# A cross-attention and feed-forward kernel: x is also loaded transposed and normed on VectorE in that layout

## The chip, the cores and the metric

The kernel runs on one core of a Trainium2 chip. The metric is the device time of one execution in microseconds (us). TensorE (PE) multiplies matrices, VectorE (DVE), ScalarE (ACT) and GpSimd (POOL) work element by element, and SyncE (SP) issues most of the DMA transfers.

## The reference, cut to what matters

```python
x = x + xattn(layernorm(x), ctx, ctx, gate_w, gate_b, outnorm_w)   # x, ctx: (16, 256, 256)
x = x + ffn(layernorm(x), w1, w2, h1, h2, w3, ...)
def layernorm(x):
    m = mean(x, -1); v = var(x, -1)
    return (x - m) / sqrt(v + 1e-5)
# xattn: q = layernorm(x), k = v = ctx, 8 heads of 32; input and forget gates from
#   [q, k, v] @ gate_w.T, a decay matrix from the gates (cumulative sum, running maximum),
#   scores = q k^T / sqrt(32) * decay; h = scores @ v / denominator; rms norm per head
# ffn: silu(x w1) * (x w2), then two layers gelu(h @ H) of 1024 x 1024, then w3 back to 256
```

## The kernel before

The 16 sequences are worked off as eight pairs of 512 tokens. `batch(i)` runs the feed-forward part of pair i: `swiglu` (w1 and w2), the first hidden layer (layer 0, eight column groups m), the second hidden layer (layer 1, again eight groups) and `project` (w3). Between its matrix products it carries two more stages: the attention of pair j = i + 1, and the preparation of pair g = i + 2 (first norm, transposition, gate products, scans). So the preparation runs in six batches, for the pairs 2 to 7; the pairs 0 and 1 ("plain") are prepared in a prologue of their own, and the last two batches have none.

Every hidden product is made twice, with a high part of the activations (a copy in a rounded 32-bit format, made by ScalarE) and a low part (the difference, made by VectorE: `lo(i, layer, m)`, line L1169). The product of layer 1 over chunk k needs `lo(i, 0, k)`.

The order on each engine is the order in which the program is written; engines meet only at semaphores. In a batch that prepares pair g the places that matter are these, in the order of time:

- VectorE, in the loop over m of layer 0: after `lo(i,0,3)` the statistics of x of pair g (tile `z`, tokens on partitions: 128 partitions x 4 token tiles x 256 features), after `lo(i,0,4)` the reciprocal root and the norm itself (L901, `z` in place), after m = 5 `take_state`, after m = 6 `take_far` (L1016), which waits for TensorE's `read_state` (L1539, the product of the transposed queries `zT` of pair j with the state).
- After `lo(i,0,7)` VectorE has `take_num` (L1023) and then one long chain for pair j: `mix_divide` (L1104 on), `mix_square`, `mix_rsqrt`, `residual`, the statistics of the second norm, `lo(i,1,0)`, `lo(i,1,1)`, the second norm, `lo(i,1,2)`, and `add_gate_low` (L926), which gives ScalarE the gates of pair g.
- ScalarE makes the tanh and the softplus of the gates (L633 to L645), with two table loads, and only then `gelu(1,4)` and its high part (L757). VectorE takes `lo(i,1,4)`, the running maximum (L953) and the offsets (L960 to L962) behind that.
- TensorE turns `z` of pair g into PSUM within layer 1, after chunk k = 3 (`turn_z`, eight products of 128 x 128, L1341, with `ident` and `z`). After the last group of layer 1 stand `turn_z2(j)` (L1341 again, with `num`) and `turn_rows(g)` (L1469), which waits for the offsets of the scan (L962), and behind them `project` (L1641, L1642).
- ScalarE copies the turned z to `zT` (L616) and again as its high part `normed_hi` (L622). GpSimd makes the low parts `keys_lo` (L549) and `normed_lo` (L553).

Six such batches have a period of 90.9 us each.

Of the kernel before, what the change touches and what calls it, by code (L numbers as in the profile page):

```python
# [7 lines left out]
ALU = mybir.AluOpType  # L8
ACT = mybir.ActivationFunctionType
AX = mybir.AxisListType  # L10
F32 = mybir.dt.float32
# [4 lines left out]
P = 128  # L16
# [54 lines left out]
SMAT_STEPS = W * ROWGRP  # L71


def build(nc, x, ctx_tok, ctx_t, gate_w, gate_b, outnorm_w, w_cols, scales, w3_s, out):
    with ExitStack() as stack:
        def sb(name, shape, dt=F32):
            return stack.enter_context(nc.sbuf_tensor(name, shape, dt))

        def sem(name):
            return stack.enter_context(nc.semaphore(name))  # L80

        x1_kept = nc.dram_tensor("x1_kept", [PAIRS, P, Q, DIM], F32, kind="Internal").ap()
        m_rows = nc.dram_tensor("m_rows", [BH, SEQ], F32, kind="Internal").ap()

        wgt = sb("wgt", [P, COLS], F32R)
        h_hi = [sb(f"h_hi{n}", [P, KH, NT], F32R) for n in range(2)]
# [43 lines left out]
        stats = sb("stats", [P, Q, 6])  # L130
        mv = sb("mv", [P, Q, 2])
        minus_mean = sb("minus_mean", [P, Q])
        nw = sb("nw", [P, 4, Q])
        rms = sb("rms", [P, 4, Q * HEADS])
        den = sb("den", [P, 2, Q * HEADS])
# [60 lines left out]
        s_ctxT = [sem(f"s_ctxT{n}") for n in range(2)]  # L196
        s_v = sem("s_v")
        s_norm1 = sem("s_norm1")
        s_z = sem("s_z")
        s_zT = sem("s_zT")  # L200
        s_zTe = sem("s_zTe")
# [54 lines left out]
        def first(j):  # L256
            return isinstance(j, int) and j == 0

        def zT(j):
            return work[:, 0:CH] if first(j) else zT_buf[:]  # L260

        def ctxT(j):
            return work[:, CH:2 * CH] if first(j) else ctxT_buf[:]

        def plain(j):

            return j < W
# [88 lines left out]
        @block.sync  # L356
        def _(sp):
            def load_z(j):
                sp.wait_ge(s_zT, j)
                sp.dma_start(z[:], x[j]).then_inc(s_zin, 16)  # L360

            def load_ctxT(j):
                reuse(sp, s_qk, W * j if j > 1 else 0)
                sp.dma_start(ctxT(j), ctx_t[j]).then_inc(s_ctxT[j % 2], 16)

            def load_v(j):
                reuse(sp, s_pv, Q * j)
                reuse(sp, s_kwt, j)
                sp.dma_start(v_aug[:], ctx_tok[j]).then_inc(s_v, 16)
# [63 lines left out]
            for i in range(PAIRS):  # L433
                j, g = i + 1, i + 2
                if j < PAIRS and j > 1:
                    load_x(j)
                if g < PAIRS:
                    load_z(g)
                    load_ctxT(g)
                    load_v(g)  # L440
                if j < PAIRS:
                    keep_x1(j)
                if g < PAIRS:
                    keep_rows(g)
                    spread_max(g)
                if i == PAIRS - 2:
                    for n in range(COMPARED_BEFORE_LAST + RAW):
                        load_raw(n)
                if i == PAIRS - 1:
                    for n in range(COMPARED_BEFORE_LAST + RAW, UNITS):  # L450
                        load_raw(n)
                    store_last(i)
                else:
                    store(i)
# [32 lines left out]
        def _(pool):  # L487
# [36 lines left out]
            def weigh_keys(j):  # L524

                pool.wait_ge(s_ecols, j + 1)
                pool.wait_ge(s_v, 16 * j + 16)
                reuse(pool, s_z2T, j)
                for b in range(W):
                    w = e_cols[:, 0, 1, b * HEADS:(b + 1) * HEADS].rearrange("p (h o) -> p h o", o=1).to_broadcast([P, HEADS, DH])  # L530
                    last = pool.tensor_tensor(k_wt[:, b], v_aug[:, b * TILES, :, 0:DH], w, ALU.mult)
                last.then_inc(s_kwt, 1)
# [11 lines left out]
                    dst = gained.rearrange("p (q h d) -> p q h d", q=Q, h=HEADS)[:, q]  # L544
                    pool.tensor_tensor(dst, src, gain, ALU.mult).then_inc(s_gained, 1)

            def split_keys_low(j):
                pool.wait_ge(s_keys_hi, j - W + 1)
                pool.tensor_tensor(keys_lo, ctxT(j), keys_hi.bitcast(F32), ALU.subtract).then_inc(s_keys_lo, 1)  # L549

            def split_normed_low(j):
                pool.wait_ge(s_zhi, j - W + 1)
                pool.tensor_tensor(normed_lo, zT(j), normed_hi.bitcast(F32), ALU.subtract).then_inc(s_zlo, 1)  # L553

            pool.memset(ident[:], 0.0).then_inc(s_ident, 1)
            pool.memset(head_mask[:], SCORE_SCALE).then_inc(s_ident, 1)
            pool.memset(future[:], 0.0).then_inc(s_ident, 1)
# [23 lines left out]
            pool.tensor_scalar(gain_b[:], gain_b[:], 1.0, None, ALU.add).then_inc(s_gain, 1)  # L581
            first_gain()
            load_weights((5, 6, 7, 8))
            for i in range(PAIRS):
                j, g = i + 1, i + 2
                if j < PAIRS:
                    weigh_keys(j)
                if g < PAIRS:
                    split_keys_low(g)
                    split_normed_low(g)  # L590

            def general_path(i):
                pool.sem_inc(s_alone, 1)
# [4 lines left out]
        def _(act):  # L598
# [8 lines left out]
            def take_zT(j):  # L607
                source = ps_a[:, 0:CH]
                if first(j):
                    act.wait_ge(s_zT_first, 1)  # L610
                    act.activation(zT(j)[:, 0], source[:, 0], ACT.Copy).then_inc(s_zTe_first, 1)
                    act.wait_ge(s_zT, 1)
                    act.activation(zT(j)[:, 1], source[:, 1], ACT.Copy).then_inc(s_zTe, 1)
                    return
                act.wait_ge(s_zT, j + 1)
                act.activation(zT(j), source, ACT.Copy).then_inc(s_zTe, 1)  # L616
                if plain(j):
                    return
                reuse(act, s_gate, j)
                if j >= 2:  # L620
                    act.wait_ge(s_mm, 2 * KH * (j - 2) + KH)
                act.activation(normed_hi, source, ACT.Copy).then_inc(s_zhi, 1)  # L622

            def take_gate_low(j):
                act.wait_ge(s_gate, j + 1)
# [208 lines left out]
        def _(dve):  # L834
# [78 lines left out]
            def norm_1_apply(j):  # L913
                if plain(j):
                    dve.wait_ge(s_zT, j)
                norm_apply(j, xs[j] if plain(j) else z, z, s_z)

            def norm_2_stats(j, src):
                norm_stats(s_norm2, j, src)
# [307 lines left out]
            def batch(i, a_stage, g_stage, last=False):  # L1227
                j, g = i + 1, i + 2
                for m in range(KH):
                    swiglu(i, m)  # L1230
                    if first(i) and m < W:
                        keep_first_x1(m)
                    if m >= 1:
                        lo_1(i, m - 1)
                lo_1(i, KH - 1)
                if a_stage:
                    masks(j)
                    floors(j)
                    weigh_scores(j, 0)
                for m in range(KH):  # L1240
                    lo(i, 0, m)
                    if a_stage and m == 1:
                        weigh_scores(j, 1)
                    if g_stage and m == 3:
                        norm_1_stats(g)
                    if g_stage and m == 4:
                        norm_rsqrt(s_norm1, g)
                        norm_1_apply(g)
                    if a_stage and m == 5:
                        take_state(j)  # L1250
                    if a_stage and m == 6:
                        take_far(j)
                    if a_stage and m == 7:
                        take_num(j)
                        mix_divide(j)
                    if last:
                        compare(COMPARED_BEFORE_LAST + m)
                if a_stage:
                    mix_square(j)
                    mix_rsqrt(j)  # L1260
                    residual(j)
                    norm_2_stats(j, xs[j % 2])
                for m in range(KH):
                    lo(i, 1, m)
                    if a_stage and m == 1:
                        norm_rsqrt(s_norm2, j)
                        norm_2_apply(j, xs[j % 2])
                    if g_stage and m == 2:
                        add_gate_low(g)
                    if g_stage and m == 3:  # L1270
                        scan_f(g)
                        shift_g(g)
                    if g_stage and m == 4:
                        scan_m(g)
                    if last:
                        compare(COMPARED_BEFORE_LAST + KH + m)
                    elif a_stage and not g_stage and m >= KH - COMPARED_BEFORE_LAST:
                        compare(m - KH + COMPARED_BEFORE_LAST)
                if last:
                    sum_inexact()  # L1280
                if a_stage:
                    take_z2T(j)
                if last:
                    finish_last(i)
                else:
                    finish(i)
# [50 lines left out]
        def _(pe):  # L1337
# [323 lines left out]
            def batch(i, a_stage, g_stage, as_is=False, last=False):  # L1661
# [38 lines left out]
                    pass  # L1700

                def between_3(k):
                    if g_stage and k == 3:
                        turn_z(g)

                def within_3(m):
                    pass
# [115 lines left out]
```

## Time and profile before

| | |
|---|---|
| median of 3 runs | 764.79 us (764.64 to 765.4) |
| the profiled execution, its own time | 764.41 us |
| span of its profile | 762.7 us |
| TensorE busy | 754.7 us, 99% of the span |
| VectorE busy | 543.6 us, 71% |
| ScalarE busy | 384.1 us, 50% |
| GpSimd busy | 53.7 us, 7% |
| granted TensorE clock | 0.999 of full speed |

Busy time is the time in which an engine executes instructions. TensorE's products overlap (one takes 0.39 us, the next starts 0.23 us later), so what one costs is read from the distance between starts and not from its duration. The time of an execution is 1.7 us more than its span.

### The profile page before, as it was taken

How to read it: one execution, taken by the hardware profiler on the slowest of the kernel's cores; microseconds unless marked ns; L12 is line 12 of the kernel's file. 1: busy time of each engine (PE TensorE's matmuls, PEld its weight loads, DVE VectorE, ACT ScalarE, POOL GpSimd, SP SyncE). 2: the span in 40 equal slices, each digit the busy share in tenths (PEclk: the TensorE clock that was granted, in tenths of full speed). 3: DMA queues.
4: the chain of work that ended last, by engine and by line, in shares of the span. 5: the costliest groups of instructions: out<-in, count | busy, mean ns of one | idle time of the engine just before them, and what ended most of it. 6: DMA issues, size and time to landing. Idle time of an engine off the chain costs nothing.

```text
span 762.7 us, 15214 instructions
## 1 busy us (share of the span) xinstructions
PE 754.7 (99%) x6296; PEld 631.7 (83%) x6296; DVE 543.6 (71%) x1295; ACT 384.1 (50%) x577; POOL 53.7 (7%) x67
## 2 busy tenths in 40 slices
PE   8999999999999999999999999999999999999998
PEld 4778888888898888988888888888889888898887
DVE  6788786696957868588676877658695784965554
ACT  3566456463365634556454554646335562445332
POOL 3400020000100020000200002000020000000000
PEclk9999999999999999999999999999999999999999
DMA  9393112200022000310005001230102100540640
GB/s 327 98 426 110 35 52 88 108 29 30 29 112 83 29 31 28 140 56 29 31 29 193 0 31 39 87 127 23 37 29 112 55 1 3 172 160 11 177 144 30
DMA packets 14617, 63.46 MB, mean 83 GB/s; under 512 B 2016, under 2 KB 2896, under 8 KB 11728
## 3 DMA queue, kind: packets, MB, share of 16 engines
q1 hardware_dynamic: 12960, 50.12, 18.9%
q0 software_dynamic: 1296, 11.53, 3.9%
q8 instruction: 51, 0.84, 0.4%
q10 hardware_dynamic: 288, 0.79, 0.3%
q14 instruction: 22, 0.18, 0.1%
HBM read 53.94 MB, written 8.50 MB: 82 GB/s over the span
## 4 chain that ended last, share of the span: by engine, by line
PE 94%; DVE 1%; ACT 0%; issue 0%
PE ps_f L1601 31%; PE ps_f L1602 30%; PE ps_f L1566 8%; PE ps_f L1567 8%; PE ps_f L1641 4%; PE ps_f L1642 4%; PE ps_a L1506 2%; PE ps_a L1489 2%; PE ps_a L1341 1%; PE ps_a L1539 1%; PE ps_a L1462 1%; PE ps_a L1455 1%; PE ps_a L1498 0%; PE ps_f L1576 0%; DVE stats L1063 0%; DVE z L1050 0%
## 5 line engine op out<-in xcount | busy, mean ns | idle before, releaser
L1601 PE MATMUL ps_f<-h_hi,wgt 128*128 128x512 f32 x1024 | 401.5, 392 | 0.0
L1602 PE MATMUL ps_f<-h_lo,wgt 128*128 128x512 f32 x1024 | 398.7, 389 | 0.0
L1601 PEld LDWEIGHTS ps_f<-h_hi,wgt 128*128 128x128 f32 x1024 | 192.2, 188 | 40.5
L1602 PEld LDWEIGHTS ps_f<-h_lo,wgt 128*128 128x128 f32 x1024 | 192.3, 188 | 39.0
L752 ACT ACTIVATE work<-ps_f,scl 128x512 f32<-128x512 f32 x128 | 87.5, 684 | 164.9 <-PE ps_f L1602 164.3
L1169 DVE TENSOR_TENSOR h_lo<-work,h_hi 128x512 fp32r<-128x512 f32 x128 | 86.6, 690 | 101.7 <-ACT h_hi L757 100.6
L1566 PE MATMUL ps_f<-h_hi,wgt 128*128 128x512 f32 x252 | 99.1, 393 | 0.0
L1567 PE MATMUL ps_f<-h_lo,wgt 128*128 128x512 f32 x252 | 98.3, 390 | 0.0
L739 ACT ACTIVATE work<-ps_f,scl 128x512 f32<-128x512 f32 x64 | 44.2, 690 | 88.2 <-PE ps_f L1567 87.5
L757 ACT ACTIVATE h_hi<-work 128x512 fp32r<-128x512 f32 x128 | 81.0, 633 | 4.1
L1160 DVE SCALAR_TENSOR_TENSOR work<-ps_f,scl,work 128x512 f32<-128x512 f32 x64 | 48.1, 751 | 39.4 <-PE ps_f L1567 37.9
L985 DVE SCALAR_TENSOR_TENSOR decay<-decay,cols,future 128x128 f32<-128x128 f32 x224 | 64.5, 366 | 0.0
L1641 PE MATMUL ps_f<-wgt,h_hi 128*128 128x256 f32 x256 | 62.4, 285 | 0.0
L1642 PE MATMUL ps_f<-wgt,h_lo 128*128 128x256 f32 x256 | 61.8, 283 | 0.0
L1566 PEld LDWEIGHTS ps_f<-h_hi,wgt 128*128 128x128 f32 x252 | 47.3, 188 | 10.6 <-DVE work L1160 0.4
L1567 PEld LDWEIGHTS ps_f<-h_lo,wgt 128*128 128x128 f32 x252 | 47.3, 188 | 9.4
L1642 PEld LDWEIGHTS ps_f<-wgt,h_lo 128*128 128x128 f32 x256 | 49.1, 192 | 0.0
L1641 PEld LDWEIGHTS ps_f<-wgt,h_hi 128*128 128x128 f32 x256 | 49.0, 192 | 0.1
L665 ACT ACTIVATE decay<-decay 128x1024 f32<-128x1024 f32 x28 | 29.7, 1062 | 35.3 <-DVE decay L985 35.3
L1165 DVE TENSOR_TENSOR h_lo<-work,h_hi 128x512 fp32r<-128x512 f32 x64 | 43.7, 683 | 0.8
L743 ACT ACTIVATE h_hi<-work 128x512 fp32r<-128x512 f32 x64 | 39.9, 624 | 4.4 <-DVE work L1160 4.3
L1001 DVE SCALAR_TENSOR_TENSOR decay<-ps_a,decay 128x512 f32<-128x512 f32 x60 | 37.2, 683 | 1.1 <-PE ps_a L1489 1.1
(214 smaller groups left out, 685.2 us busy)
## 6 DMA issues: line engine op xcount, KB each, us to landing
decay<-m_rows SPq DMA_DIRECT2D x14, 1024.0 KB, 6.6
decay<-w_cols SPq DMA_DIRECT2D x22, 512.0 KB, 4.2
wgt<-w_cols POOLq DMA_DIRECT2D x5, 1024.0 KB, 11.8
v_aug<-ctx_tok SPq DMA_DIRECT2D x8, 528.0 KB, 3.9
wgt<-w_cols POOLq DMA_DIRECT2D x2, 2048.0 KB, 14.1
x_kept<-xs SPq DMA_DIRECT2D x8, 512.0 KB, 2.6
xs<-x SPq DMA_DIRECT2D x7, 512.0 KB, 3.6
ctxT<-ctx_t SPq DMA_DIRECT2D x7, 512.0 KB, 3.3
```

Source lines behind the costliest of these rows:

```text
L739: act.activation(work[:, m % 2], ps_f[:, bank], ACT.Silu, scale=scl[:, 0, m:m + 1]).then_inc(s_silu, 1)
L752: act.activation(work[:, m % GELU], ps_f[:, (turn_of(i) + m) % 4], ACT.Gelu, scale=scl[:, 2 + layer, m:m + 1]).then_inc(s_gelu, 1)
L757: act.activation(h_hi[1 - layer][:, m], work[:, m % GELU], ACT.Copy).then_inc(s_hi, 1)
L985: last = dve.scalar_tensor_tensor(part, part, cols[:, t, row:row + 1], future[:], ALU.subtract, ALU.add)
L1160: dve.scalar_tensor_tensor(work[:, 2 + m % 2], ps_f[:, bank], scl[:, 1, m:m + 1], work[:, m % 2], ALU.mult, ALU.mult).then_inc(s_hf, 1)
L1169: dve.tensor_tensor(h_lo[1 - layer][:, m], work[:, m % GELU], h_hi[1 - layer][:, m].bitcast(F32), ALU.subtract).then_inc(s_lo, 1)
L1566: pe.matmul(ps_f[:, bank + half], w, moving(z2_hi[:, c], as_is), start=(c == 0), stop=False)
L1567: last = pe.matmul(ps_f[:, bank + half], w, moving(z2_lo[:, c], as_is), start=False, stop=(c == CH - 1))
L1601: pe.matmul(ps_f[:, bank], w, moving(h_hi[layer][:, k], as_is), start=(k == 0), stop=False)
L1602: last = pe.matmul(ps_f[:, bank], w, moving(h_lo[layer][:, k], as_is), start=False, stop=(k == KH - 1))
L1641: pe.matmul(to, moving(h_hi[0][:, k, q * P:(q + 1) * P], as_is), w, start=(k == 0), stop=False)
L1642: last = pe.matmul(to, moving(h_lo[0][:, k, q * P:(q + 1) * P], as_is), w, start=False, stop=(k == KH - 1))
```

## The change

From pair 2 on, x comes from HBM a second time, already transposed (`x_t`, features on partitions, made on the host), and straight into `zT`. VectorE still takes the statistics from `z`. It then keeps mean and reciprocal root of the 512 tokens in `moments`; one DMA writes them to HBM and another spreads them over all 128 partitions into `z`, whose contents are no longer needed. In the transposed layout these are one value for each column, so VectorE subtracts and multiplies with two tensor-tensor operations over 1024 elements for each partition. The low parts move from GpSimd to VectorE, `turn_z` and ScalarE's copy to `zT` go, and `normed_hi` is now read from `zT`.

```diff
+        def moment_spread(k):
+            per_token = z[:].rearrange("p q d -> p (q d)").rearrange("p (k t q) -> p k q t", k=2, q=Q)[:, k]
+            return per_token.rearrange("p (o q) t -> p o q t", o=1).to_broadcast([P, CH, Q, P])
+        def by_tile(a):
+            return a.rearrange("p c (q t) -> p c q t", q=Q)
...
# SyncE
+            def spread_moments(j):
+                sp.wait_ge(s_moments, j - W + 1)
+                reuse(sp, s_moments_in, 16 * (j - W))
+                sp.dma_start(moment_rows.rearrange("k p q -> p k q"), moments[:]).then_inc(s_moments_out, 16)
+                sp.wait_ge(s_moments_out, 16 * (j - W) + 16)
+                sp.dma_start(z[:].rearrange("p q d -> p (q d)"),
+                             moment_rows.rearrange("(o k) p q -> o (k p q)", o=1).to_broadcast([P, 2 * NT])).then_inc(s_moments_in, 16)
+            def load_xT(j):
+                sp.wait_ge(s_farmm, j)
+                sp.dma_start(zT(j), x_t[j]).then_inc(s_xT, 16)
...
                     load_z(g)
                     load_ctxT(g)
+                    spread_moments(g)
+                    load_xT(g)
                     load_v(g)
...
# ScalarE, take_zT, from pair 2 on
-                act.wait_ge(s_zT, j + 1)
-                act.activation(zT(j), source, ACT.Copy).then_inc(s_zTe, 1)
+                act.wait_ge(s_zTe, j + 1)
...
-                act.activation(normed_hi, source, ACT.Copy).then_inc(s_zhi, 1)
+                act.activation(normed_hi, zT(j), ACT.Copy).then_inc(s_zhi, 1)
...
# VectorE
+            def keep_moments(j):
+                reuse(dve, s_moments_out, 16 * (j - W))
+                dve.tensor_copy(moments[:, 0], mv[:, :, 0])
+                dve.tensor_copy(moments[:, 1], nw[:, 3, 0:Q]).then_inc(s_moments, 1)
+            def norm_in_place(j):
+                dve.wait_ge(s_moments_in, 16 * (j - W) + 16)
+                dve.wait_ge(s_xT, 16 * (j - W) + 16)
+                dve.tensor_tensor(by_tile(zT(j)), by_tile(zT(j)), moment_spread(0), ALU.subtract).then_inc(s_xT_centred, 1)
+                dve.wait_ge(s_xT_centred, j - W + 1)
+                dve.tensor_tensor(by_tile(zT(j)), by_tile(zT(j)), moment_spread(1), ALU.mult).then_inc(s_zTe, 1)
...
                     if g_stage and m == 4:
                         norm_rsqrt(s_norm1, g)
-                        norm_1_apply(g)
+                        keep_moments(g)
                     if a_stage and m == 5:
                         take_state(j)
                     if a_stage and m == 6:
                         take_far(j)
+                    if g_stage and m == 6:
+                        norm_in_place(g)
                     if a_stage and m == 7:
                         take_num(j)
+                        if g_stage:
+                            split_keys_low(g)
+                            split_normed_low(g)
                         mix_divide(j)
...
# TensorE
                 def between_3(k):
-                    if g_stage and k == 3:
-                        turn_z(g)
+                    pass
```

How the rows stand on the engines that wait or are waited for, for one batch that prepares a pair (the six read alike):

VectorE before, from `take_state` (L1008) to the mixing of pair j (L1104 and on):

```order
L1008 TENSOR_TENSOR state<-ps_a,head_mask 128x528
L1169 TENSOR_TENSOR h_lo<-work,h_hi 128x512
L1016 TENSOR_TENSOR state<-ps_a,e_cols 128x528
L1169 TENSOR_TENSOR h_lo<-work,h_hi 128x512
L1023 TENSOR_TENSOR num<-ps_a,state 128x2x264
L1104 SCALAR_TENSOR_TENSOR den<-num 128x32
L1105 SCALAR_TENSOR_TENSOR den<-den,floor 128x32
```

VectorE of the changed kernel at the same place (L1053, L1214, L1061, L1068 and L1149 are the old L1008, L1169, L1016, L1023 and L1104):

```order
L1053 TENSOR_TENSOR state<-ps_a,head_mask 128x528
L1214 TENSOR_TENSOR h_lo<-work,h_hi 128x512
L1061 TENSOR_TENSOR state<-ps_a,e_cols 128x528
L951 TENSOR_TENSOR zT<-zT,z 128x1024
L953 TENSOR_TENSOR zT<-zT,z 128x1024
L1214 TENSOR_TENSOR h_lo<-work,h_hi 128x512
L1068 TENSOR_TENSOR num<-ps_a,state 128x2x264
L957 TENSOR_TENSOR h_lo<-ctxT,h_hi 128x1024
L961 TENSOR_TENSOR h_lo<-zT,h_hi 128x1024
L1149 SCALAR_TENSOR_TENSOR den<-num 128x32
```

Four operations over 1024 elements now stand between `take_far` and the mixing, two of them ahead of `lo(i,0,7)`.

SyncE's queue before, for one pair (a load of z, then the transposed keys, the values, the store of x1):

```order
L360 DMA z<-x 128x1024
L364 DMA ctxT<-ctx_t 128x1024
L369 DMA v_aug<-ctx_tok 128x1056
L396 DMA x_kept<-xs 128x1024
```

SyncE's queue of the changed kernel at the same place:

```order
L380 DMA z<-x 128x1024
L397 DMA ctxT<-ctx_t 128x1024
L386 DMA moment_rows<-moments 128x2x4
L388 DMA z<-moment_rows 128x1024
L393 DMA zT<-x_t 128x1024
L402 DMA v_aug<-ctx_tok 128x1056
L429 DMA x_kept<-xs 128x1024
```

Three transfers, each with a wait in front of it, now stand ahead of the load of the values.

## Rows read from the trace of the kernel before

**Rows 1.** The page: busy time and instructions, and granted clock by slices

```profile
PE 754.7 (99%) x6296; PEld 631.7 (83%) x6296; DVE 543.6 (71%) x1295; ACT 384.1 (50%) x577; POOL 53.7 (7%) x67
...
PEclk9999999999999999999999999999999999999999
```

**Rows 2.** Timeline of PE, third batch: start, duration, line, tiles, count

```profile
273.30 1.06 PE L1539 MATMUL ps_a<-state,zT 128*128 128x132 f32 x8
...
280.90 0.39 PE L1602 MATMUL ps_f<-h_lo,wgt 128*128 128x512 f32 x1
281.14 1.03 PE L1341 MATMUL ps_a<-ident,z 128*128 128x128 f32 x8
281.93 0.48 PE L1601 MATMUL ps_f<-h_hi,wgt 128*128 128x512 f32 x1
282.24 0.40 PE L1602 MATMUL ps_f<-h_lo,wgt 128*128 128x512 f32 x1
...
284.75 0.39 PE L1601 MATMUL ps_f<-h_hi,wgt 128*128 128x512 f32 x1
```

**Rows 3.** Timeline of PE behind layer 1, third batch and sixth

```profile
309.30 1.03 PE L1341 MATMUL ps_a<-ident,num 128*128 128x128 f32 x8
310.17 0.30 PE L1469 MATMUL ps_a<-ident,rows 80*128 80x80 f32 x2
...
582.83 0.30 PE L1469 MATMUL ps_a<-ident,rows 80*128 80x80 f32 x2
```

**Rows 4.** Timeline of DVE, third batch, last row of the sixth

```profile
274.40 0.71 DVE L1016 TENSOR_TENSOR state<-ps_a,e_cols 128x528 f32<-128x528 f32 x1 [0.63 <-PE ps_a L1539]
279.09 0.69 DVE L1169 TENSOR_TENSOR h_lo<-work,h_hi 128x512 fp32r<-128x512 f32 x1 [3.98 <-ACT h_hi L757]
279.70 0.70 DVE L1023 TENSOR_TENSOR num<-ps_a,state 128x528 f32<-128x528 f32 x1
280.49 2.06 DVE L1104 SCALAR_TENSOR_TENSOR den<-num 128x32 f32<-128x32 f32 x1
...
285.71 1.02 DVE L1115 TENSOR_TENSOR rms<-rms,den 128x32 f32<-128x32 f32 x1
...
301.18 0.41 DVE L926 TENSOR_TENSOR decay<-ps_a,decay 48x256 f32<-48x256 f32 x1
...
307.08 0.69 DVE L1169 TENSOR_TENSOR h_lo<-work,h_hi 128x512 fp32r<-128x512 f32 x1 [1.61 <-ACT h_hi L757]
...
309.05 0.27 DVE L962 TENSOR_SCALAR rows<-state 16x128 f32<-16x128 f32 x1
...
581.67 0.27 DVE L962 TENSOR_SCALAR rows<-state 16x128 f32<-16x128 f32 x1
```

**Rows 5.** Timeline of ACT, third batch, behind the gates

```profile
301.62 0.51 ACT L633 ACTIVATE rows<-decay,gb 48x256 f32<-48x256 f32 x1 [5.27 <-DVE decay L926]
...
306.35 0.63 ACT L757 ACTIVATE h_hi<-work 128x512 fp32r<-128x512 f32 x1
```

**Rows 6.** Timeline of POOL, third batch

```profile
280.09 2.39 POOL L549 TENSOR_TENSOR h_lo<-ctxT,h_hi 128x1024 fp32r<-128x1024 f32 x1 [32.28 <-ACT h_hi L605]
```

**Rows 7.** Timeline of DVE in the seventh batch, which prepares no pair

```profile
644.04 0.22 DVE L1104 SCALAR_TENSOR_TENSOR den<-num 128x32 f32<-128x32 f32 x1
644.29 0.19 DVE L1105 SCALAR_TENSOR_TENSOR den<-den,floor 128x32 f32<-128x32 f32 x1
...
647.42 0.19 DVE L1115 TENSOR_TENSOR rms<-rms,den 128x32 f32<-128x32 f32 x1
```

**Rows 8.** Groups by line and form, DVE: count, busy us, mean ns

```profile
L1134 DVE TENSOR_TENSOR num<-num,gain_b 128x1024 f32<-128x1024 f32 x7 | 8.6, 1225 | 0.2
...
L851 DVE SCALAR_TENSOR_TENSOR nw<-nw 128x4 f32<-128x4 f32 x42 | 6.8, 163 | 1.4
```

**Rows 9.** Line L364, the load of the transposed keys (512 KB)

```profile
DMA to landing us min/median/max: 3.1/3.3/6.8
```

**Rows 10.** DMA issues by line: count, KB, median us to landing

```profile
z<-x SPq DMA_DIRECT2D x6, 512.0 KB, 4.5
...
m_rows<-state SPq DMA_DIRECT2D x7, 16.0 KB, 1.4
```

More of the change, by code:

```diff
@@ L71, with build @@
 SMAT_STEPS = W * ROWGRP
-def build(nc, x, ctx_tok, ctx_t, gate_w, gate_b, outnorm_w, w_cols, scales, w3_s, out):
+def build(nc, x, x_t, ctx_tok, ctx_t, gate_w, gate_b, outnorm_w, w_cols, scales, w3_s, out):
     with ExitStack() as stack:
@@ L83, in build @@
         m_rows = nc.dram_tensor("m_rows", [BH, SEQ], F32, kind="Internal").ap()
+        moment_rows = nc.dram_tensor("moment_rows", [2, P, Q], F32, kind="Internal").ap()
         wgt = sb("wgt", [P, COLS], F32R)
@@ L132, in build @@
         minus_mean = sb("minus_mean", [P, Q])
+        moments = sb("moments", [P, 2, Q])
         nw = sb("nw", [P, 4, Q])
@@ L198, in build @@
         s_norm1 = sem("s_norm1")
+        s_moments = sem("s_moments")
+        s_moments_out = sem("s_moments_out")
+        s_moments_in = sem("s_moments_in")
+        s_xT = sem("s_xT")
+        s_xT_centred = sem("s_xT_centred")
         s_z = sem("s_z")
@@ L358, in load_z @@
             def load_z(j):
-                sp.wait_ge(s_zT, j)
+                if j > W:
+                    sp.wait_ge(s_zTe, j)
+                else:
+                    sp.wait_ge(s_zT, j)
                 sp.dma_start(z[:], x[j]).then_inc(s_zin, 16)
+            def spread_moments(j):
[8 more added lines that the diff above has]
+                sp.dma_start(zT(j), x_t[j]).then_inc(s_xT, 16)
             def load_ctxT(j):
@@ L545, in first_gain @@
                     pool.tensor_tensor(dst, src, gain, ALU.mult).then_inc(s_gained, 1)
[L547 to L553, printed above, removed]
             pool.memset(ident[:], 0.0).then_inc(s_ident, 1)
@@ L583, in _ @@
             load_weights((5, 6, 7, 8))
[L584 to L590, printed above, removed]
+            for j in range(1, PAIRS):
+                weigh_keys(j)
             def general_path(i):
@@ L614, in take_zT @@
                     return
-                act.wait_ge(s_zT, j + 1)
-                act.activation(zT(j), source, ACT.Copy).then_inc(s_zTe, 1)
                 if plain(j):
+                    act.wait_ge(s_zT, j + 1)
+                    act.activation(zT(j), source, ACT.Copy).then_inc(s_zTe, 1)
                     return
+                act.wait_ge(s_zTe, j + 1)
                 reuse(act, s_gate, j)
@@ L915, in norm_1_apply, with split_keys_low, split_normed_low @@
                     dve.wait_ge(s_zT, j)
-                norm_apply(j, xs[j] if plain(j) else z, z, s_z)
+                norm_apply(j, xs[j], z, s_z)
+            def keep_moments(j):
[8 more added lines that the diff above has]
+                dve.tensor_tensor(by_tile(zT(j)), by_tile(zT(j)), moment_spread(1), ALU.mult).then_inc(s_zTe, 1)
+            def split_keys_low(j):
+                dve.wait_ge(s_keys_hi, j - W + 1)
+                dve.tensor_tensor(keys_lo, ctxT(j), keys_hi.bitcast(F32), ALU.subtract).then_inc(s_keys_lo, 1)
+            def split_normed_low(j):
+                dve.wait_ge(s_zhi, j - W + 1)
+                dve.tensor_tensor(normed_lo, zT(j), normed_hi.bitcast(F32), ALU.subtract).then_inc(s_zlo, 1)
             def norm_2_stats(j, src):
@@ L1789 @@
     ctx_t = np.ascontiguousarray(ctx.reshape(PAIRS, NT, CH, P).transpose(0, 3, 2, 1))
+    x_t = np.ascontiguousarray(np.asarray(x).reshape(PAIRS, NT, CH, P).transpose(0, 3, 2, 1))
     def up(w):
@@ L1812 @@
     arrays = {
-        "x": tok(x), "ctx_tok": v_aug, "ctx_t": ctx_t, "gate_w": gate_w, "gate_b": gate_b,
+        "x": tok(x), "x_t": x_t, "ctx_tok": v_aug, "ctx_t": ctx_t, "gate_w": gate_w, "gate_b": gate_b,
         "outnorm_w": np.ascontiguousarray(np.asarray(L0_xattn_outnorm_w).reshape(1, DIM)),
```

## The prediction

> **What bounds the kernel now.** I read the page first: TensorE is busy for 99% of the span, at the full clock in every slice [rows 1]. So only what TensorE no longer does, or a new wait of TensorE, can move the time. I then read TensorE's timeline in the third batch, where the change takes its eight transpositions out [rows 2], and the place where TensorE comes nearest to waiting, which is behind layer 1 [rows 3]. There `turn_rows` starts at 310.17, and the VectorE row that it needs, L962, ends at 309.05 + 0.27 = 309.32 [rows 4]. The slack is 0.85 us. In the sixth batch it is the same: 582.83 less 581.94 gives 0.89 [rows 3, 4].
>
> What feeds L962 is one rigid chain, and I followed it backwards. L953 and the offsets stand behind `lo(i,1,4)` (307.08), which waited 1.61 us for ScalarE's high part. That one stands behind the softplus, and the first step of it, L633 at 301.62, had waited 5.27 us for VectorE's L926 [rows 4, 5]. From 279.70 to L926 at 301.18 VectorE's rows follow each other with no idle time named. So every microsecond by which `mix_divide` (L1104) starts later, less what VectorE saves on the way to L926, arrives at `turn_rows`; 0.85 of it is free.
>
> **What the change removes.** On TensorE, `turn_z`. The product L1602 at 282.24 would have started at 281.13 + 0.23 = 281.36 with nothing between (neighbouring starts are 0.23 apart). Eight transpositions cost 0.88 us, six times 5.3 us [rows 2]. On ScalarE one copy of 1024 elements goes; ScalarE is not in the chain before L926, so this is worth nothing. On VectorE the norm of z goes, and two copies of four elements come (0.16 us each by their size [rows 8]). That stretch ends in waits of VectorE for ScalarE and TensorE (0.63 and 3.98 us [rows 4]), so it is worth nothing either. On GpSimd the two low parts go. The first runs from 280.09 to 282.48 [rows 6], and VectorE's L1104, which starts in it, takes 2.06 us; L1115 takes 1.02. In the seventh batch, where GpSimd has no low parts, the same lines take 0.22 and 0.19 [rows 4, 7]. From L1104 to L1115 it is 5.22 us against 3.38, and with L1115's own 0.83 the chain gets 2.67 us back.
>
> **What it adds ahead of L1104.** The order is: `take_far`, wait for x transposed, two operations, `lo(i,0,7)`, `take_num`, two low parts, L1104.
>
> 1. The load of x transposed can only be issued when `read_state` has read `zT`; VectorE's L1016 waits for the same event and starts at 274.40 [rows 4]. A load of this size and layout lands 3.3 us after its issue (3.1 at least) [rows 9]. With 0.05 for SyncE to wake, VectorE starts at 277.75. Nothing hides this: VectorE would else have waited for `lo(i,0,7)` until 279.09, so the wait itself costs nothing, but what comes behind it does.
> 2. Two operations over 1024 elements. An ordinary one takes 1.225 us [rows 8]. These read `z` at a step of four elements (mean and root lie as token by tile, and the innermost loop goes over tokens). No row shows that step. The nearest is L1104 in the seventh batch, which reads every 33rd element: 0.222 us for 32 elements, where L1105, with 32 neighbouring ones, takes 0.19. Four elements take 0.163 [rows 7, 8], so a neighbouring element costs about 1.04 ns and the fixed part is 0.159, while the strided one costs (222 - 159) / 32 = 1.97 ns. At this price an operation takes 0.159 + 1024 x 0.00197 = 2.18 us. Bounds: 1.225 and 2.18. I take 2.18, since the row with a stride is nearer to this access than rows without one. With 0.05 between them: 4.41 us, to 282.16.
> 3. `lo(i,0,7)` 0.61 and `take_num` 0.79, from start to start [rows 4]: 283.56.
> 4. Two low parts at 1.225, overlapping by 0.1 each as `lo` does (0.69 long, 0.61 apart): 2.26, to 285.82.
>
> L1104 starts 5.33 us later than 280.49. Less 2.67: the chain arrives 2.66 us later. The slack takes 0.85, so `turn_rows` starts 1.81 us later than now, and I add 0.1 for TensorE to start again. TensorE itself gets there 0.88 earlier, but this gain only makes its wait longer (2.7 us). For six pairs: 6 x 1.9 = 11.4 us. The two bounds of item 2 give 1.9 and 0 for a pair.
>
> The Trainium skill has a rule that speaks against this access, in "SBUF — State Buffer", section "Door 1: The DMA port swizzle": SBUF is read in lines of 16 bytes, and an access that goes on to a new line each time pays. A step of four fp32 is just 16 bytes, so by this every element would pay; the page gives no price, and at the row's price the sum stays as above. The same paragraph also calls a stride of up to 4 fp32 free; by that reading the sum would be 0 for a pair. No row of this trace has the step itself.
>
> **What else could stop.** `lo(i,0,7)` now ends at about 282.85; TensorE needs it for chunk 7 of layer 1, at 284.75 now and 0.88 earlier without `turn_z`, 283.87 [rows 2]. One microsecond is left. `normed_hi` on ScalarE follows the second operation and is done a microsecond before VectorE asks for it. The moments are ready about 269; a small write lands in 1.4 us and a 512 KB load in up to 4.5 [rows 10], about 275 in all, before x lands at 277.7. The load of the values is issued later by one issue only.
>
> **The rivals.**
>
> - *The strided reads run at full rate.* Then the chain is 2.66 - 1.91 = 0.75 late, within the slack, but TensorE now also arrives 0.88 earlier and waits for the same L962: 0.1 us saved for a pair at best. 764.2 to 764.8 us, no change that can be told. For it: VectorE's 32-element rows are short, and their 30 ns could come from something other than the stride. Chance 0.15.
> - *Faster: the chain is early enough and TensorE keeps its 0.88 for each pair.* 764.8 - 5.3 = 759.5. It needs the chain to be no later than now: full rate, and x landing 0.75 us sooner than the median, 2.55 us from issue. The fastest of the seven is 3.1 [rows 9]. Chance 0.05.
> - *A longer stall than mine:* the moments come last (their write goes out in 256 pieces of 16 bytes, no row shows such a write), or the load of x shares the engines with the spread or the values and takes 4.5 us, as z does [rows 10]. This adds 1.2 us for a pair, 7 us in all: 783. Or the granted clock falls in the new gaps of 2.7 us: it is full in all slices now [rows 1], and if it were down to the lower level for as long as the gap lasts, 2.7 us of products would take 5.4, 16 us in all: 792. Chance together 0.08. The skill's page "TensorE: Matmul & The Clock Gate", section "Why this matters for your kernels", warns of idle gaps; no gap in this trace is followed by a lower clock.
> - *The forecast:* 0.72.
>
> **The numbers.** The sum of 11.4 is made on the profiled execution (764.41, 0.4 under the median); on the median, 764.8 + 11.4 = 776.2 us. The likeliest case alone, with x landing between 3.1 and 4.1 us and the price of a strided element between 1.8 and 2.1 ns: 773.5 to 781. The range reaches down to the full-rate case: 764 to 781. A change of over 0.2% (1.5 us) can be told from none here. Faster 0.06 (the second rival and a tail of the first), within 0.2% 0.13, slower 0.81.
>
> **What would show it.** In the new profile L951 and L953 take 2.2 us each (1.2 if I am wrong), preceded by about 2.7 us of idle time released by the load of x. L1104's counterpart takes 0.22 in all batches. TensorE has a wait of about 2.7 us before the transposed rows in six batches, put down to VectorE's offsets, some 16 us in all, and no transposition of `z` behind the prologue. The period of six batches grows from 90.9 to about 92.8 us. What would make it wrong: the two operations at 1.2 us; another wait in that chain, at the moments; or a shift that dies out before L926 because VectorE had idle time there that I did not see.

## The result, and the profile after

The changed kernel takes 783.29 us in the median of four runs (781.81 to 785.17), the kernel before 764.78 beside it: the ratio is 1.0242, 95% interval 1.0213 to 1.027. It is 18.5 us slower. The forecast was 776.2 us, with a range from 764 to 781: the direction was right, the size too small, and the time lies outside the range. The profiled execution is the slowest of the four (785.17 us), with a span of 783.4 us, 20.7 more than before.

The page of the changed kernel, busy time and granted clock by slices, beside [rows 1]:

```profile
PE 758.1 (97%) x6248; PEld 633.0 (81%) x6248; DVE 556.8 (71%) x1307; ACT 378.1 (48%) x571; POOL 24.7 (3%) x55
...
PEclk9999999999999999999999999999998999999999
```

VectorE has 13 us more to do, TensorE 48 products fewer. The clock line has one 8 in it, which is easily passed over. The waits of the changed kernel (who waited for whom, total us, times, longest):

```profile
ACT rows L656 <- DVE decay L971: 54.1, 6, 9.5
...
DVE zT L951 <- DMA zT<-x_t: 21.8, 6, 4.5
...
PE ps_a L1519 <- DVE rows L1007: 16.6, 6, 3.2
```

These are the three links of the chain that the prediction named: VectorE waits for x transposed, ScalarE's softplus waits longer for VectorE, and TensorE waits for the scan, now six times and 2.8 us each. The same links in VectorE's timeline, third batch, beside [rows 4]:

```profile
277.65 0.71 DVE L1061 TENSOR_TENSOR state<-ps_a,e_cols 128x528 f32<-128x528 f32 x1 [0.63 <-PE ps_a L1589]
282.82 1.99 DVE L951 TENSOR_TENSOR zT<-zT,z 128x1024 f32<-128x1024 f32 x1 [4.46 <-DMA zT<-x_t]
284.84 1.98 DVE L953 TENSOR_TENSOR zT<-zT,z 128x1024 f32<-128x1024 f32 x1
286.74 0.68 DVE L1214 TENSOR_TENSOR h_lo<-work,h_hi 128x512 fp32r<-128x512 f32 x1
...
287.96 1.21 DVE L957 TENSOR_TENSOR h_lo<-ctxT,h_hi 128x1024 fp32r<-128x1024 f32 x1
289.10 1.22 DVE L961 TENSOR_TENSOR h_lo<-zT,h_hi 128x1024 fp32r<-128x1024 f32 x1
290.23 0.22 DVE L1149 SCALAR_TENSOR_TENSOR den<-num 128x32 f32<-128x32 f32 x1
...
308.24 0.41 DVE L971 TENSOR_TENSOR decay<-ps_a,decay 48x256 f32<-48x256 f32 x1
...
316.10 0.27 DVE L1007 TENSOR_SCALAR rows<-state 16x128 f32<-16x128 f32 x1
```

From L1061 to L1149 it is 12.58 us, where the old lines L1016 to L1104 lie 6.09 apart. From L1149 to L971 it is 18.01 against 20.69: the 2.7 us that GpSimd's low parts used to cost. And TensorE at the place of [rows 3], batches one and three:

```profile
126.45 1.03 PE L1391 MATMUL ps_a<-ident,num 128*128 128x128 f32 x8
129.83 0.36 PE L1519 MATMUL ps_a<-ident,rows 80*128 80x80 f32 x2 [2.34 <-DVE rows L1007]
...
130.31 0.28 PE L1691 MATMUL ps_f<-wgt,h_hi 128*128 128x256 f32 x1
130.42 0.28 PE L1692 MATMUL ps_f<-wgt,h_lo 128*128 128x256 f32 x1
...
312.17 1.04 PE L1391 MATMUL ps_a<-ident,num 128*128 128x128 f32 x8
316.42 0.53 PE L1519 MATMUL ps_a<-ident,rows 80*128 80x80 f32 x2 [3.21 <-DVE rows L1007]
...
317.47 0.41 PE L1692 MATMUL ps_f<-wgt,h_lo 128*128 128x256 f32 x1
317.68 0.41 PE L1691 MATMUL ps_f<-wgt,h_hi 128*128 128x256 f32 x1
```

In the first batch the products of `project` follow each other at 0.12 us, in the third at 0.21. The windows of the same stretches (stretch, its length, PE busy, count, granted clock, share of the DMA engines, GB/s) say why:

```profile
130.00:138.00 8.00, 8.00 (x68) 1.00 0.69 264
316.50:320.00 3.50, 3.50 (x18) 0.54 0.64 213
320.00:326.00 6.00, 6.00 (x51) 1.00 0.56 228
600.60:605.00 4.40, 4.40 (x22) 0.50 0.62 253
```

A granted clock of 0.50 is the lower level, 1.2 GHz. TensorE had stood still for 3.2 us before 316.42 and for 2.8 before the same place of the sixth batch, 600.49. `project` takes 7.63 us from its first product to its last in batches one and two, as before, and 8.99, 9.11, 9.12 and 10.14 in the batches three to six: 6.8 us more in all.

So the periods of the six batches, from one `read_state` to the next, are 92.6, 92.6, 95.4, 94.3, 95.3 and 95.7 us, where they were 90.89. That is 20.5 us, nearly the whole difference of the spans. It comes apart as follows. The six distances from L1061 to L1149 are 11.22, 11.28, 12.58, 11.44, 12.44 and 11.72. Less 6.09 each they sum to 34.1; less 2.7 each for what GpSimd no longer costs, and less the 0.85 of slack, 12.8 are left. The slower `project` is 6.8. The remaining 0.9 is TensorE starting again: it starts 0.06 us behind the end of L1007, and from the transposed rows to `project` it is 0.15 us in four of these batches and 0.26 in two, where it was 0.10 before.

### The profile page after: what moved, and what is told of

Read it like the earlier page. It is cut to its first block, busy times and chain, and to the rows that moved or that the text cites. A ratio compares the mean times of both kernels' runs of the same rounds, so it can differ in the third digit from the quotient of the medians.

```text
span 783.4 us, 15134 instructions
## 1 busy us (share of the span) xinstructions
PE 758.1 (97%) x6248; PEld 633.0 (81%) x6248; DVE 556.8 (71%) x1307; ACT 378.1 (48%) x571; POOL 24.7 (3%) x55
## 4 chain that ended last, share of the span: by engine, by line
PE 65%; DVE 20%; issue 4%; ACT 3%; DMA 3%; DVEq 0%; ACTq 0%
PE ps_f L1651 18%; PE ps_f L1652 18%; PE ps_f L1616 8%; PE ps_f L1617 7%; PE ps_f L1691 4%; PE ps_f L1692 4%; DMA zT<-x_t 3%; DVE h_lo L1214 3%; PE ps_a L1539 2%; DVE zT L951 2%; PE ps_a L1556 1%; DVE stats L909 1%; ACT L775 1%; ACT L660 1%; DVE xs L1184 1%
## 5 line engine op out<-in xcount | busy, mean ns | idle before, releaser
L1214 DVE TENSOR_TENSOR h_lo<-work,h_hi 128x512 fp32r<-128x512 f32 x128 | 86.5, 689 | 84.2 <-ACT h_hi L780 82.8
L1691 PE MATMUL ps_f<-wgt,h_hi 128*128 128x256 f32 x256 | 68.9, 305 | 0.0
L1692 PE MATMUL ps_f<-wgt,h_lo 128*128 128x256 f32 x256 | 67.9, 301 | 0.0
L1691 PEld LDWEIGHTS ps_f<-wgt,h_hi 128*128 128x128 f32 x256 | 54.2, 212 | 0.1
L1692 PEld LDWEIGHTS ps_f<-wgt,h_lo 128*128 128x128 f32 x256 | 54.1, 211 | 0.0
```

Source lines behind the costliest of these rows:

```text
L1214: dve.tensor_tensor(h_lo[1 - layer][:, m], work[:, m % GELU], h_hi[1 - layer][:, m].bitcast(F32), ALU.subtract).then_inc(s_lo, 1)
L1691: pe.matmul(to, moving(h_hi[0][:, k, q * P:(q + 1) * P], as_is), w, start=(k == 0), stop=False)
L1692: last = pe.matmul(to, moving(h_lo[0][:, k, q * P:(q + 1) * P], as_is), w, start=False, stop=(k == KH - 1))
```

## The experiments

The theory (A) is that nothing but this chain costs time: it starts when x lands, carries two operations that are slow because of their stride, is charged one to one beyond 0.85 us of slack, and beyond some length of TensorE's gap the clock adds its own part. Ten kernels ran, each beside the kernel before on the same chip.

**The gap filled.** Sixteen filler products between `turn_z2` and `turn_rows`:

```diff
                     if g_stage and m == 7:
+                        keep_clock(16, ps_a[:, 3])
                         turn_rows(g)
```

> The changed kernel with 16 products of 128 columns (ident by ident, into an unused bank) between turn_z2 and turn_rows, some 1.8 us of the gap in which TensorE waits for the scan. Theory A (the clock: TensorE's gap of 2.3 to 3.2 us lets the granted clock fall in four of six batches, and project then runs at the lower level for a time): the clock stays at 1.00, project's products are 0.12 us apart in all batches, the chain is as late as before, and the time falls by some 7 us to about 776. Theory B (project's slow products come from the transfers that run beside them): no change, 782 to 785.

785.20 us (783.81 to 786.46), which is neither. The filler took twice what I had worked out; each of its 16 products stands in the trace as two rows:

```profile
221.65 3.74 PE L1769 MATMUL ps_a<-ident 128*128 128x128 f32 x32
225.22 0.30 PE L1519 MATMUL ps_a<-ident,rows 80*128 80x80 f32 x2
```

It was longer than the gaps of the changed kernel (2.3 to 3.2 us), so it was a stall itself. But `project` took 7.64 us in all six batches, with the transfers running as before. That already speaks against theory B; the time did not decide it. The six periods are 20.4 us longer than before. Of these 16.1 are six times the 2.7 us by which the shortest of them (93.57) exceeds 90.89, that is the filler less the saved transpositions; 0.9 is TensorE waiting in two batches for `lo(i,0,7)`; and most of the rest are two pauses of 0.8 and 2.2 us in the middle of the products of L1556, for which the profile names no cause.

**A shorter filler.** Six products instead of 16:

> The changed kernel with 6 filler products instead of 16 ahead of turn_rows. In the first filler run 16 of them took 3.7 us, more than the gap, so they were a stall of their own; 6 should take 1.4 us and fit into the gap of 2.3 to 3.4 us. Theory A (the clock's fall costs some 7.5 us of the 18.5): project takes 7.6 us in all six batches and the time is 775 to 779. Theory B (not the clock): 782 to 785.

778.73 us (777.23 to 779.95), 4.6 less than the changed kernel. The filler took 1.50 us and a wait of 0.9 to 1.8 us was left behind it. `project` took 7.6 us in five batches and 9.13 in one. So the clock's part is real, and most of it comes back when TensorE has something to do in the gap. That it falls once even so, behind a wait of 1.82 us, is one reason why the gain is less than 6.8; a pause of 1.3 us at L1556, again with no cause named, is another.

**Neighbouring moments.** z is loaded for the statistics with tokens 4p to 4p+3 on partition p, so that the moments come out in token order:

```diff
-                sp.dma_start(z[:], x[j]).then_inc(s_zin, 16)
+                sp.dma_start(z[:], x_n[j]).then_inc(s_zin, 16)
...
-.rearrange("p (k t q) -> p k q t", k=2, q=Q)[:, k]
+.rearrange("p (k q t) -> p k q t", k=2, q=Q)[:, k]
...
+        "x_n": np.ascontiguousarray(np.asarray(x).reshape(PAIRS, P, Q, DIM)),
```

> The changed kernel, but z for the statistics is loaded with tokens 4p to 4p+3 on partition p (one more array of the host), so that the spread mean and root lie in token order and L951 and L953 read neighbouring elements; all else alike. Theory A (the step of four elements costs the 0.8 us by which each of the two is longer than 1.22): they take 1.22 us each, the chain is 1.6 us earlier in six batches (9.6 us), TensorE's gaps shrink to 0.7 to 1.6 us and the clock does not fall (some 7 us more): about 766. Rival (they are long because they work in place, or beside a transfer): still 2.0 us, 783.

770.47 us (769.57 to 771.34), ratio 1.0067 (1.005 to 1.0084). The two lines, first in the changed kernel and then in this one (ns minimum/median/maximum):

```profile
L951 DVE TENSOR_TENSOR zT<-zT,z x6: 1992/2027/2049, 96.2 to 566.9; 128x1024 f32<-128x1024 f32 x6
```

```profile
L951 DVE TENSOR_TENSOR zT<-zT,z x6: 1226/1226/1226, 97.0 to 557.3; 128x1024 f32<-128x1024 f32 x6
```

In the same place, in the same layout of the output, beside the same transfers, only the step of one operand differs: 0.80 us of 2.03 is the stride. The rival is out. The time is 4.5 us above what I expected, because x still landed 5.2 and 5.4 us after its issue in two batches, and behind one of them the clock fell once (9.12 us for `project`).

**The last reader of zT earlier.** `read_state` stands after column group 6 instead of within group 7:

```diff
                         values(j, 0, 0)
                         values(j, 0, 1)
+                    if a_stage and m == 6:
+                        read_state(j)
...
                     if a_stage and m == 7:
-                        read_state(j)
                         values(j, 1, 0)
```

> The changed kernel with read_state, the last reader of zT, after column group 6 of layer 0 instead of within group 7, some 1.8 us earlier. Theory A (the chain starts when x transposed lands, and that is set by the issue behind read_state): L951 starts 1.8 us earlier in six batches (10.8 us), the clock does not fall: about 765. Rival (the spread of the moments or the engines of the DMA hold x back): less than 4 us, about 780.

768.57 us (768.27 to 769.51), ratio 1.0048 (1.0031 to 1.0065), with the clock full throughout. The issue is 1.8 us earlier, but the load now runs beside the spread of the moments and lands 4.2 to 4.6 us after it, so L951 starts only 0.9 us earlier in the first batch. The rest of the gain is that no batch has x as late as 5.1 us and none loses its clock. So both expectations held in part: the issue behind `read_state` sets the start, and x takes longer when the spread lands 2.3 to 3.0 us behind its issue. That the spread is what holds it back is argued: no run took it away with the early issue, and in the second batch of the changed kernel, where the two overlap by 1.0 us, x landed after 3.74 us as elsewhere.

**Both edits together.**

> The changed kernel with both edits: z loaded so that the moments lie in token order (L951 and L953 at 1.23 us), and read_state after column group 6. Theory A (the chain to turn_rows is the whole loss, and its terms add): the chain is a further 1.5 us earlier than with read_state alone, TensorE's gap of 1.5 us closes, and the 0.88 us of the transpositions that went is kept: periods of 90.0 to 90.2 us, about 760 (759.5 to 761.5). Rival (the saved 0.88 us is spent on another wait, or x still lands late in some batches): 763 to 766.

759.54 us (759.32 to 760.48), ratio to the kernel before 0.9931 (0.9917 to 0.9944): faster than both. TensorE at the place of [rows 3]:

```profile
306.44 1.03 PE L1391 MATMUL ps_a<-ident,num 128*128 128x128 f32 x8
307.31 0.30 PE L1519 MATMUL ps_a<-ident,rows 80*128 80x80 f32 x2
307.41 0.36 PE L1691 MATMUL ps_f<-wgt,h_hi 128*128 128x256 f32 x1
```

and VectorE's end of the chain ahead of it:

```profile
306.77 0.27 DVE L1007 TENSOR_SCALAR rows<-state 16x128 f32<-16x128 f32 x1
```

No wait is named any more, and the slack is 0.27 us here and 0.09 to 0.47 in the six batches. The distance from one of these places to the next is 90.01 us, 0.88 under the old period, which is the price of the eight transpositions as [rows 2] gave it.

**The low parts back on GpSimd.** The two subtractions moved back to GpSimd's queue as they were, everything else as changed:

```diff
# GpSimd
+                if g < PAIRS:
+                    split_keys_low(g)
+                    split_normed_low(g)
...
# VectorE
                         take_num(j)
-                        if g_stage:
-                            split_keys_low(g)
-                            split_normed_low(g)
                         mix_divide(j)
```

> The changed kernel with the two low parts back on GpSimd, everything else as changed. Theory A (their move gives VectorE's chain 2.26 us of work and takes 2.67 us of slowed instructions away, so it was no loss): the chain is 0.4 us later or unchanged, 783 to 787. Rival (the low parts on VectorE are what makes the chain late): some 2 us for each pair less and no fall of the clock, 765 to 770.

797.19 us (793.83 to 798.33): slower by 14 us still, more than either expectation. The move to VectorE was a gain. VectorE, second batch, and GpSimd beside it:

```profile
195.01 4.09 DVE L966 TENSOR_TENSOR zT<-zT,z 128x1024 f32<-128x1024 f32 x1
199.01 0.69 DVE L1219 TENSOR_TENSOR h_lo<-work,h_hi 128x512 fp32r<-128x512 f32 x1
...
200.41 2.35 DVE L1154 SCALAR_TENSOR_TENSOR den<-num 128x32 f32<-128x32 f32 x1
```

```profile
194.85 2.40 POOL L584 TENSOR_TENSOR h_lo<-ctxT,h_hi 128x1024 fp32r<-128x1024 f32 x1 [32.27 <-ACT h_hi L640]
200.26 2.41 POOL L588 TENSOR_TENSOR h_lo<-zT,h_hi 128x1024 fp32r<-128x1024 f32 x1 [3.01 <-ACT h_hi L658]
```

The multiplication takes 4.1 us instead of 2.0 while GpSimd runs, and the next row, `lo(i,0,7)`, is late for chunk 7: TensorE waits for it 8.8 us in all, besides 16.2 for the scan. The clock falls more often too: `project` takes 9.1 us in five batches, and in the fourth and fifth the clock falls a second time, at the waits of 2.3 and 2.1 us for that low part.

```profile
PE ps_a L1521 <- DVE rows L1012: 16.2, 6, 3.2
PE ps_f L1653 <- DVE h_lo L1219: 8.8, 6, 2.3
```

**Why x lands late in some batches.** It lands 3.7 to 5.1 us after its issue, and not in the same batches from kernel to kernel. First the load of the values, issued 1.25 us behind it, goes behind the store of x1:

```diff
                     load_xT(g)
-                    load_v(g)
                 if j < PAIRS:
                     keep_x1(j)
+                if g < PAIRS:
+                    load_v(g)
```

> The changed kernel, but SyncE loads the values after the store of x1 instead of 1.25 us behind the load of x transposed. If the two share the engines and this is why x lands 3.7 to 5.1 us after its issue: L951 starts at most 3.8 us behind the issue in all six batches, 3 us of chain less and fewer falls of the clock: 774 to 780. If not: x still lands up to 5.1 us, 782 to 785.

781.67 us (780.36 to 784.76). Then the two transfers of the moments are left out, and with them the waits for them:

```diff
                     load_ctxT(g)
-                    spread_moments(g)
                     load_xT(g)
```

> The changed kernel without the two small transfers of the moments: L951 and L953 read what lies in z, so that the normed x of pairs 2 to 7 is not that of the reference. It asks whether the spread, which lands just as the load of x transposed is issued, is what makes x land late in some batches. If so: x lands at most 3.7 us after its issue in all six, the chain is 3 to 5 us shorter in sum and the clock falls less often, 773 to 779. If not: x still lands up to 5.1 us in some, 781 to 785.

781.70 us (779.68 to 782.50). The load of x transposed in the two kernels, the one without the values behind it first:

```profile
DMA to landing us min/median/max: 3.6/3.8/5.1
```

```profile
DMA to landing us min/median/max: 3.7/3.7/4.9
```

Neither of them alone is the reason; both at once were not taken away. The records of the single transfers say more. The load consists of 128 packets of 4 KB, and the last of them usually starts 2.9 to 3.2 us after the issue. In the fourth batch of the kernel without the values behind it (issue at 370.06, landing 5.1 us later) a packet of 16 KB, of a queue that the profile calls `instruction`, starts at 373.10 and takes 0.88 us. In the stretches 373.10 to 373.20, 373.36 to 373.96 and 373.96 to 374.45:

```profile
q8 instruction: 1, 0.02, 55.0%
...
DMA packets 0, 0.00 MB, mean 0 GB/s; under 512 B 0, under 2 KB 0, under 8 KB 0
...
DMA packets 2, 0.00 MB, mean 8 GB/s; under 512 B 1, under 2 KB 1, under 8 KB 2
```

For 0.6 us nothing starts; then, as the packet of 16 KB ends, come the last 4 KB of x and the 4 bytes behind them. The same stands in the other kernels. With `read_state` in its old place there are 42 loads of x in seven kernels. The 12 that landed 4.7 to 5.4 us after their issue and the six at 4.0 to 4.3 each have a packet that starts within 0.02 us of the end of such an instruction packet; the 24 that landed after 3.4 to 3.9 us have none, though an instruction packet runs beside 22 of them as well. So a load is late when one of its packets stands behind an instruction packet. This is read from the traces; no run moved or removed such a packet.

**The dose, on the kernel before.** The chain is made late on purpose by one or three operations over 1024 elements, their results unused, in the six batches that prepare a pair; the transpositions stay in:

```diff
+            def spend(n):
+                for _ in range(n):
+                    dve.tensor_tensor(h_sq, h_sq, h_sq, ALU.mult).then_inc(s_spent, 1)
+                    spent[0] += 1
+                    dve.wait_ge(s_spent, spent[0])
...
                     mix_square(j)
+                    if g_stage:
+                        spend(1)        # 3 in the second kernel
                     mix_rsqrt(j)
```

> The kernel before, with one more operation over 1024 elements (1.26 us from start to start, its result unused) in VectorE's chain ahead of mix_rsqrt, in the six batches that prepare a pair. Theory A (0.85 us of lateness are free, the rest arrives at turn_rows one to one, without a fall of the clock for a gap this short): 0.4 to 0.5 us for a pair, 2.5 to 3 us in all, 767.7. Rival (the chain has more slack than 0.85 us): 765.

767.69 us (767.47 to 768.26), ratio 1.0037 (1.0024 to 1.005). Expected were 767.7. The periods are 91.4 us, 0.5 more than before: 1.26 less 0.85 of slack, and 0.1 to start again. TensorE's wait for the scan is 1.5 us in all, six times.

> The kernel before with three more such operations (3.78 us) in each of the six batches. Theory A: 3.78 less 0.85 is 2.93 us for a pair, 17.6 us in all, and TensorE's gap of 2.9 us lets the clock fall behind it in some batches, 1.5 us each: 783 with no fall, up to 792 with a fall in all six. Rival (a gap costs no more than itself): 782.5 to 783.5 and project at 7.6 us in every batch.

790.86 us (790.28 to 791.78), ratio 1.0345 (1.0327 to 1.0364). The first batch has a period of 93.9 us and `project` at 7.64; the five others have 95.4 and 9.12. In the windows behind the gap of the third batch (gap first, then three of 3 us):

```profile
316.00:320.00 4.00, 2.01 (x14) 1.00 0.01 2
321.00:324.00 3.00, 3.00 (x17) 0.53 0.61 205
324.00:327.00 3.00, 3.00 (x25) 0.90 1.02 423
327.00:330.00 3.00, 3.00 (x28) 1.00 0.17 71
```

This kernel has no new transfer and no strided operation. A gap of 2.8 us costs 3.0 us by itself and 1.5 more where the clock falls behind it.

## Why the prediction was right and where it was wrong

- **The place and the chain: right.** TensorE waits at `turn_rows` for VectorE's offsets in six batches, and behind the prologue nowhere else for more than 0.3 us. The microsecond left for `lo(i,0,7)` was used up in the third batch, where x is latest: TensorE waits 0.21 us for it (to 287.48), which the wait behind it hides. The slack of 0.85 us and the one to one behind it are shown by the kernels with one and three more operations. The saved transpositions are worth 0.88 us for a pair, and are only seen when the wait is gone.
- **The strided operations: right in kind.** Worked out from a 32-element row: 2.18 us each. Measured: 2.03 and 1.98. The shift is 0.45 us for a pair less than I had, 2.7 us in all. The rule of the Trainium skill ("SBUF — State Buffer", section "Door 1: The DMA port swizzle") that an access going to a new line of 16 bytes each time pays agrees with the trace: 2.03 us with the step of 16 bytes, 1.226 with none. Its other reading, that 4 fp32 are free, does not.
- **The low parts: right.** 2.27 us for the two against 2.26 expected; L1149 takes 0.22 in all batches, and 2.7 us come back. `take_num` is followed 0.61 later, not 0.79, as nothing waits for its result any more: 1.1 us in all.
- **When x lands: the term that was mis-sized.** The step "VectorE starts at 277.75", 3.35 us after L1016's start, rested on the load of the keys, which has the queue to itself. Measured from L1061's start to L951's: 3.76, 3.83, 5.17, 3.97, 5.02 and 4.27 us. That is 5.9 us more in six batches. I had this as a rival with 7 us; that rival and the clock had together a chance of 0.08. The reason given there, a share of the engines with the spread or the values, is not what the runs show: taking either away left the late landings, and the traces have a packet of x behind an instruction packet in each of them.
- **The clock: the step that failed.** The prediction named a fall of the clock behind gaps of 2.7 us, priced it, and left it nearly without a chance because "no gap in this trace is followed by a lower clock". That trace had no gap behind the prologue to try it on. It fell in four of six batches and cost 6.8 us of the profiled execution; the kernels with a short filler and with three more operations show it as a cost of the gap. The price was too high (16 us for all six; a fall cost 1.3 to 1.5 us, once 2.5), the chance far too low. Without this term the estimate from the trace is 764.8 + 13.7 = 778.5 us, inside the range. The Trainium skill's warning of idle gaps ("TensorE: Matmul & The Clock Gate", section "Why this matters for your kernels") agrees with the trace: the clock fell behind gaps of 2.6 to 3.2 us.

Together: 11.4 forecast, less 2.7 for the operations and 1.1 for `take_num`, and 5.9 more for x, is 13.5, where the trace has 13.7 with the restarts; with the clock's 6.8 it is 20.5. That the sum without the clock came near is in part luck: x cost 5.9 more, and two other terms 3.8 less.

## What to carry to other kernels

Work taken off the busiest engine is worth nothing when the same change makes its next wait longer. Here 0.88 us for a pair was saved and the period still grew by 1.7 to 4.8, and two edits of layout and order brought the saving back. When a forecast contains a new gap of TensorE, put the clock into the sum and not among the rivals; and when a load moves into the critical chain, price it by its slowest landings, not by the median of a load that nobody waits for. A stride set by which token lies on which partition can be removed where the data is loaded: here that was one array more and 12.8 us less (783.29 to 770.47).

## What the runs showed that I had not expected

- **Whether the clock falls does not follow from the gap's length alone.** In the changed kernel it stayed full behind gaps of 2.3 and 2.4 us and fell behind 2.6, 2.8 and 3.2. Without the spread of the moments it stayed full twice and fell twice behind the same 2.3 us. With three more operations it stayed full once and fell five times behind 2.8 us. It fell once behind 1.5 us of filler and 1.8 us of wait. With the low parts on GpSimd it fell behind a gap of 1.75 us and not behind 1.58. A fall costs 1.3 to 1.5 us in `project`, once 2.5.
- **GpSimd slows a strided operation of VectorE as it does a short one.** The multiplication over 1024 elements went from 1.98 to 4.1 us while GpSimd subtracted beside it for 2.4 us; in the kernel before, an operation of 0.22 us became one of 2.06 in the same way. It goes the other way too: with the low parts on GpSimd, in the fourth batch, VectorE's subtraction had been running for 0.5 us when GpSimd's began; it took its usual 1.99 us, and GpSimd's 3.78 instead of 2.4.
- **A 512 KB load has a tail.** With `read_state` in its old place, x lands after 3.4 to 4.3 us in most batches and 4.7 to 5.4 in one or two of six, also when the load behind it or the transfers ahead of it are taken away in turn. In every late one a packet of the load starts as an instruction packet of 16 KB, which took 0.9 to 1.8 us, ends.
